# A four-layer graph network on one core: layer 0 loads x transposed and takes its means off there

## The chip, the core and the metric

One core of one Trainium2 chip runs the whole program. The metric is the device time of one execution in microseconds (us); lower is better. The kernel before has a median of 1261.44 us in three runs (1258.7 to 1262.8).

## What is computed

x holds 128 graphs of 128 nodes with 256 features in fp32, and adj one 128x128 adjacency matrix with ones on its diagonal. Four layers follow one another, each of them x = x + layer(relu(layernorm(x))):

```python
# layer 0                                   a = adj as float, deg = a.sum(axis=1)
out = deg * (h @ Wi.T + b) + a @ (h @ Wj.T)
# layer 1                                   Wh = h @ W
logits = leaky_relu(Wh @ a_src + (Wh @ a_dst).T); out = softmax(masked logits) @ Wh
# layer 2                                   the same with 128 columns, and h itself beside it
# layer 3                                   8 heads of 32: softmax(masked q @ k.T / sqrt(32)) @ v, then @ Wo.T + bo
```

Layernorm has no weights: (x - mean) / sqrt(var + 1e-5) over the 256 features. Adjacency is the same for all graphs.

## The kernel before

The graphs are worked on in 64 pairs (G = 2); p is the number of a pair. A pair passes through some 120 operations on five engines. Each engine runs `step(t)` for t from -31 on, and in it a fixed list of operations, each on pair t - LAG[operation]. An operation waits by semaphores for what it reads, for the readers of the buffer it overwrites (`read_before`), and on TensorE for the earlier readers of its PSUM bank (`bank_free`, from the table BANKS). Nothing else orders the engines: each takes its list strictly in order, so one that waits holds up all that stands behind it in its list. LAG counts list rounds of an engine by itself, not time.

Layer 0 of a pair, in order: SyncE loads x (`load`). VectorE takes statistics (`stats0`, L486, and `mv0`, L495). GpSimd makes var + eps, its power -0.5 and the negative mean (`veps0` L311, `rstd0` L327, `nm0` L317), and the normalised rows `y0` (L335, two instructions). TensorE transposes them in four pieces of 128x128 (`h0t`, L911) into one bank. ScalarE applies relu and rounds to fp32r (`h0t_hi`, L726), and VectorE keeps what the rounding left (`h0t_lo`, L524). TensorE multiplies by both weights with three products each (`m0`, `m1`, L901 to L903). ScalarE and VectorE split the neighbours' half the same way (`mj_hi` L732, `mj_lo` L502), VectorE adds deg times the own half to x + deg * b (`t0_0`, `t0_1`, L509; GpSimd's `r0`, L343), and TensorE multiplies by the adjacency (`s0`, L930), after which VectorE sums (`x1`).

Layer 1 needs the products with a_dst along a row. GpSimd gathers the column (`dst1`, L358) once ScalarE has copied the projections (`wh0`, `wh1`, L738). SyncE writes it to DRAM (`row_out1`, L251: rows<-dst) and, when that has landed, reads it back spread over all partitions (`row_in1`, L257: db<-rows). ScalarE then forms the logits (`z1`, L764), VectorE masks them (`nmax1`, L534), ScalarE takes the exponentials (`exp1`, L773), TensorE transposes them (`e1t`, L966), ScalarE copies (`at1`, L781), and TensorE attends (`x2_mm`, L974). Layer 2 has the same round through DRAM (`dst2`, `row_out2`, `row_in2`, `z2`). The first four and last five pairs go without DRAM: TensorE spreads the column by two transposes of a broadcast column (`d1`, `d2`, L958).

ScalarE's list before, from `z1` on: z1, ht2, p3t_0, p3t_2, p3t_3, exp1, hh, h1t_hi, exp3_3, at1, ot_hi, h0t_hi, exp3_1, wh0, wh1, p3t_1, h3t_hi, v, z2, mj_hi1, exp3_2, exp2, mj_hi0, exp3_0, at2, and z1 of the next pair. `exp3_*` are four exponentials each (L795), `p3t_*` copies of 128x512 (L803), `ot_hi` one of 128x512 (L809).

SyncE's list before: row_in1, row_out2, row_in2, load (L239), row_out1, store (L244). All of its DMAs are on one queue.

Of the kernel before, what the change touches and what calls it, by code (L numbers as in the profile page):

```python
# [29 lines left out]
       "row_in1": 1, "row_out2": 2, "row_in2": 2, "load": -4, "row_out1": 0, "store": 7, "x4_mm": 7, "products": 0, "m1": -1, "qt_mm": 4, "m0": -1,  # L30
       "kt_mm": 4, "e2t": 3, "d1": 1, "pt0": 6, "h2t": 2, "pt2": 6, "x3_mm": 3, "pt3": 6, "hh_mm": 2, "h1t": 0, "scores": 4, "adj_spread": -31,
       "ot_mm": 6, "e1t": 1, "pt1": 5, "h0t": -2, "x2_mm": 1, "wh0_mm": 0, "wh1_mm": 0, "v_mm": 4, "h3t": 3, "d2": 2, "s0": -1, "exp3_1": 5, "wh0": 1,
       "wh1": 1, "p3t_1": 6, "h3t_hi": 4, "v": 5, "w3_high": 0, "z2": 3, "w0_high": -9, "mj_hi1": -1, "exp3_2": 5, "exp2": 3, "mj_hi0": -1,
       "exp3_0": 5, "at2": 3, "z1": 1, "ht2": 2, "p3t_0": 6, "p3t_2": 6, "p3t_3": 6, "exp1": 1, "hh": 2, "h1t_hi": 0, "exp3_3": 5, "at1": 1,
       "ot_hi": 6, "h0t_hi": -2, "qt": 5, "t0_1": 0, "rsum2": 4, "stats0": -2, "mj_lo0": 0, "rsum3_1": 6, "rsum3_2": 6, "kt": 5, "rsum3_0": 6,
       "nmax1": 2, "x3": 4, "t0_0": 0, "stats3": 4, "mv3": 4, "w0_low": -1, "rsum1_any": 2, "h1t_lo": 1, "nmax3_1": 5, "adj_rows": -29, "nmax3_2": 5,
       "mv0": -2, "nmax3_0": 5, "rsum3_3": 6, "h0t_lo": -1, "ot_lo": 7, "x2": 2, "nmax3_3": 5, "stats2": 2, "h3t_lo": 4, "mv2": 2, "x1": 0,
       "nmax2": 3, "x4": 7, "stats1": 0, "mv1": 0, "w1_split": 0, "mj_lo1": -1, "y3": 4, "r0": -2, "dst1": 1, "w3_low1": 1, "w3_low3": 2, "veps0": -2,
       "nm0": -2, "p3_0": 6, "rstd0": -2, "p3_3": 6, "veps2": 2, "nm2": 2, "deg_b_made": -23, "rstd2": 2, "y2": 2, "w3_low2": 1, "veps1": 0, "r3": 5,
       "nm1": 0, "rstd1": 0, "y1": 0, "x3_tail": 3, "p3_2": 5, "p3_1": 5, "y0": -2, "dst2": 2, "veps3": 3, "nm3": 3, "w3_low0": 2, "rstd3": 3,  # L40
       "rsum1": 1,
# [4 lines left out]
    "x4b": (6, "x4_mm", ('x4',)),  # L46
    "prep": (4, "products", ('w1_split',)),
    "m1": (0, "m1", ('mj_lo1', 't0_1')),
    "qt": (1, "qt_mm", ('qt',)),
    "m0": (5, "m0", ('mj_lo0', 't0_0')),  # L50
    "kt": (6, "kt_mm", ('kt',)),
    "at2": (2, "e2t", ('at2',)),
    "d1": (4, "d1", ('z1',)),
    "pt0": (0, "pt0", ('p3t_0',)),
    "h2t": (1, "h2t", ('ht2',)),
    "pt2": (3, "pt2", ('p3t_2',)),
    "x3b": (2, "x3_mm", ('x3',)),
    "pt3": (4, "pt3", ('p3t_3',)),
    "hh": (6, "hh_mm", ('hh',)),
    "h1t": (3, "h1t", ('h1t_lo',)),  # L60
    "sc0": (1, "scores", ('nmax3_0',)),
    "sc1": (2, "scores", ('nmax3_1',)),
    "sc2": (5, "scores", ('nmax3_2',)),
    "sc3": (0, "scores", ('nmax3_3',)),
    "prepa": (0, "adj_spread", ('adj_rows',)),
    "ot": (4, "ot_mm", ('ot_lo',)),
    "at1": (6, "e1t", ('at1',)),
    "pt1": (3, "pt1", ('p3t_1',)),
    "h0t": (2, "h0t", ('h0t_lo',)),
    "x2b": (6, "x2_mm", ('x2',)),  # L70
    "wh0": (5, "wh0_mm", ('wh0',)),
    "wh1": (1, "wh1_mm", ('wh1',)),
    "v": (2, "v_mm", ('v',)),
    "h3t": (5, "h3t", ('h3t_lo',)),
    "d2": (4, "d2", ('z2',)),
    "x1b": (3, "s0", ('x1',)),
# [6 lines left out]
BUFFERS = {"x0": 2, "y0": 2, "ht0": 2, "mj": 2, "t0": 2, "r0": 2, "x1": 2, "y1": 2, "ht1": 2, "wh": 2, "z1": 2, "e1": 2, "at1": 2, "x2": 2, "y2": 2, "ht2": 2, "hh": 2, "z2": 2, "e2": 2, "at2": 2, "x3": 2, "y3": 2, "ht3": 2, "kt": 2, "qt": 2, "v": 2, "r3": 2, "exps3": 1, "probs3": 1, "probs3t": 1, "ot": 2, "x4": 2, "masked3": 1}  # L83


def gnn_kernel(nc, x, adj, w0t, bias0, w1, w1t, a1, w2, w2t, a2, wqt, bq, wkt, bk, wvt, bv, wot, bo, out):
# [7 lines left out]
    with ExitStack() as ctx:  # L94
# [44 lines left out]
        y = [sb("y0", [P, BUFFERS["y0"], G, D]), sb("y1", [P, BUFFERS["y1"], G, D]), sb("y2", [P, BUFFERS["y2"], G, D]), sb("y3", [P, BUFFERS["y3"], G, D])]  # L139
# [25 lines left out]
        nm = [sb(f"nm{i}", [P, SMALL, G]) for i in range(4)]  # L165
# [20 lines left out]
        x_in = [sem(f"x_in{i}") for i in range(BUFFERS["x0"])]  # L186
        x_out = [sem(f"x_out{i}") for i in range(BUFFERS["x4"])]


        S = {name: sem(name) for name in LAG if name not in ("row_in1", "row_out2", "row_in2", "load", "row_out1", "store")}  # L190
# [44 lines left out]
        def _(sp):  # L235
            def load(p):
                b = p % BUFFERS["x0"]
                read_before(sp, "x0", p, "y0", "r0")
                sp.dma_start(x0[:, b], x_pairs[bass.ds(p, 1)].rearrange("o n g d -> (o n) g d")).then_inc(x_in[b], 16)  # L239

            def store(p):
                b = p % BUFFERS["x4"]
                passed(sp, "x4", p)
# [15 lines left out]
            def step(t):  # L259
# [6 lines left out]
                if due(t, "load") and t - LAG["load"] >= 2:  # L266
                    load(t - LAG["load"])
# [870 lines left out]
```

## Time and profile before

| | us |
|---|---|
| median of three runs (1258.7 to 1262.8) | 1261.44 |
| span of the profiled execution | 1270.7 |
| TensorE matmuls busy | 1244.1 (98%) |
| VectorE busy | 1073.1 (84%) |
| GpSimd busy | 1066.2 (84%) |
| ScalarE busy | 1042.1 (82%) |

The profiled execution's own time is its span; no time around it is recorded. It is 9.3 us, or 0.7%, above the median of the runs that were not profiled. TensorE's rows give for each matmul the time from its start to a modelled end; matmuls overlap, so the time that one costs is read from one start to the next, not from its duration. In the timeline and in the table of lines, "idle before" is what the engine waited directly before that instruction, and the name behind the arrow is what ended it.

### The profile page before, as it was taken

What the parts mean: (1) busy time and instruction counts of PE and PEld (TensorE: products, weight loads), DVE (VectorE), ACT (ScalarE), POOL (GpSimd) and SP (SyncE); (2) the same over time, 40 slices, a digit from 0 to 9 for tenths busy, and PEclk for the clock granted to TensorE, in tenths of its full rate; (3) what the DMA queues carried; (4) which work ended last, traced back from release to release, by engine and by line L of the source; (5) the groups of instructions that cost most, each with busy time, mean ns of one, the idle gap of its engine ahead of it and who ended that gap; (6) DMA issues with size and microseconds to landing.
All of it is one profiled execution on the core that took longest, in us unless ns stands there. A gap on an engine that the chain in (4) does not pass through costs nothing. (4 is left out here: it accounts for less than half of the span.)

```text
span 1270.7 us, 43666 instructions
## 1 busy us (share of the span) xinstructions
PE 1244.1 (98%) x12253; PEld 1143.5 (90%) x12253; DVE 1073.1 (84%) x5137; ACT 1042.1 (82%) x3911; POOL 1066.2 (84%) x1914
## 2 busy tenths in 40 slices
PE   8899999999999999999999999999999999999997
PEld 6789999999999999999899999899999989999986
DVE  5788888888988888888888888888988888888883
ACT  3578888888888888888788888788888888898996
POOL 6879888888888888888788888889888888887773
PEclk8999999999999999999999999999999999999998
DMA  4011221222222321221211222322222312211000
GB/s 127 26 23 22 52 43 36 52 36 43 52 39 40 52 45 35 51 47 32 52 32 47 48 35 48 48 34 50 48 36 47 48 31 52 48 27 31 19 19 34
DMA packets 70604, 53.59 MB, mean 42 GB/s; under 512 B 20704, under 2 KB 70368, under 8 KB 70368
## 3 DMA queue, kind: packets, MB, share of 16 engines
q1 hardware_dynamic: 67888, 49.09, 20.0%
q8 instruction: 104, 1.70, 0.7%
q14 instruction: 132, 1.08, 0.6%
q10 hardware_dynamic: 2480, 1.71, 0.5%
HBM read 33.89 MB, written 16.89 MB: 40 GB/s over the span
## 5 line engine op out<-in xcount | busy, mean ns | idle before, releaser
L795 ACT ACTIVATE exps<-masked,nmax 128x128 f32<-128x128 f32 x1024 | 397.5, 398 | 0.0
L335 POOL TENSOR_SCALAR y<-x,nm,rstd 128x256 f32<-128x256 f32 x512 | 281.0, 557 | 23.4 <-issue 21.8
L364 POOL TENSOR_TENSOR probs<-exps,rsum 128x512 f32<-128x512 f32 x256 | 263.5, 1041 | 10.4 <-PE bank L1019 5.6
L577 DVE CUSTOM_DVE_ANT_0 masked<-bank,mask 128x128 f32<-128x128 f32 x1024 | 227.8, 284 | 2.9 <-PE bank L1011 2.8
L795 ACT ACTIVATION_READ_ACCUMULATOR exps<-masked,nmax 128x1 f32 x1024 | 202.3, 198 | 0.0
L486 DVE BATCH_NORM_STATS2 stats<-x 128x6 f32<-128x256 f32 x512 | 190.8, 414 | 8.7 <-DMA x<-in_x 7.2
L901 PE MATMUL bank<-w_hi,ht_hi 128*128 128x512 f32 (+1 forms) x512 | 187.7, 367 | 2.1 <-DVE ht_lo L524 2.1
L327 POOL TENSOR_TENSOR rstd<-veps,power 128x2 f32<-128x2 f32 x256 | 182.8, 714 | 0.1
L524 DVE SCALAR_TENSOR_TENSOR ht_lo<-bank,ht_hi 128x512 fp32r<-128x512 f32 x192 | 131.0, 682 | 57.1 <-ACT ht_hi L726 56.8
L903 PE MATMUL bank<-w_hi,ht_lo 128*128 128x512 f32 (+1 forms) x512 | 175.6, 343 | 0.0
L902 PE MATMUL bank<-w_lo,ht_hi 128*128 128x512 f32 (+1 forms) x512 | 175.3, 342 | 0.0
L726 ACT ACTIVATE ht_hi<-bank 128x512 fp32r<-128x512 f32 x192 | 115.8, 603 | 71.3 <-PE bank L911 66.0
L911 PE MATMUL bank<-ident,y 128*128 128x128 f32 x1024 | 156.3, 275 | 5.0 <-POOL y L335 3.2
L1019 PE MATMUL bank<-ident,probs 128*128 128x128 f32 x1024 | 153.2, 273 | 0.6 <-DVE t L509 0.6
L803 ACT ACTIVATE probs3t<-bank 128x512 f32<-128x512 f32 x256 | 137.9, 595 | 3.4 <-PE bank L1019 3.4
L732 ACT ACTIVATE mj_hi<-bank 128x256 fp32r<-128x256 f32 x128 | 49.2, 384 | 103.0 <-PE bank L903 95.7
L911 PEld LDWEIGHTS bank<-ident,y 128*128 128x128 f32 x1024 | 116.2, 141 | 16.4 <-issue 6.4
L1019 PEld LDWEIGHTS bank<-ident,probs 128*128 128x128 f32 x1024 | 119.9, 141 | 2.0 <-issue 2.0
L903 PEld LDWEIGHTS bank<-w_hi,ht_lo 128*128 128x128 f32 x512 | 97.7, 191 | 12.1
L901 PEld LDWEIGHTS bank<-w_hi,ht_hi 128*128 128x128 f32 x512 | 97.8, 191 | 10.7 <-DVE ht_lo L524 2.6
L902 PEld LDWEIGHTS bank<-w_lo,ht_hi 128*128 128x128 f32 x512 | 97.5, 190 | 8.6
L311 POOL TENSOR_SCALAR veps<-mv 128x2 f32<-128x2 f32 x256 | 59.2, 231 | 52.2 <-DVE mv L495 31.5
(122 smaller groups left out, 3737.5 us busy)
## 6 DMA issues: line engine op xcount, KB each, us to landing
x<-in_x SPq DMA_DIRECT2D x64, 256.0 KB, 5.0
out<-x SPq DMA_DIRECT2D x64, 256.0 KB, 6.2
db<-rows SPq DMA_DIRECT2D x110, 128.0 KB, 4.1
rows<-dst SPq DMA_DIRECT2D x110, 1.0 KB, 4.1
probs<-in_w0t ACTq DMA_DIRECT2D x1, 256.0 KB, 5.6
probs<-in_w0t SPq DMA_DIRECT2D x1, 256.0 KB, 6.7
probs<-in_w1t ACTq DMA_DIRECT2D x1, 256.0 KB, 6.7
exps<-in_wot SPq DMA_DIRECT2D x1, 256.0 KB, 7.4
```

Of the source, the lines that this page charges most:

```text
L327: pool.tensor_tensor(rstd[i][:, b], veps[i][:, b], power[:], ALU.pow).then_inc(S[f"rstd{i}"], 1)
L335: last = pool.tensor_scalar(y[i][:, b, g], src[:, bx, g], nm[i][:, s, g:g + 1], rstd[i][:, s, g:g + 1], ALU.add, ALU.mult)
L364: pool.tensor_tensor(probs3[:, p % BUFFERS["probs3"], j], exps3[:, p % BUFFERS["exps3"], j], rsum3[:, s, j].unsqueeze(2).to_broadcast([P, ...
L486: last = dve.bn_stats(stats[i][:, b, g], src[:, bx, g])
L577: last = dve.tensor_tensor_reduce(masked3[:, b, j, i], bank_of(f"sc{j}")[:, i * P:(i + 1) * P], mask[:], scale=-1.0, scalar=-MASKED, op0=A ...
L795: last = act.activation(exps3[:, b, j, i], masked3[:, p % BUFFERS["masked3"], j, i], ACT.Exp, bias=nmax3[:, s, j, i:i + 1], scale=-1.0, ac ...
L803: act.activation(probs3t[:, b, j].rearrange("p b n -> p (b n)"), bank_of(f"pt{j}")[:], ACT.Copy).then_inc(S[f"p3t_{j}"], 1)
L901: pe.matmul(out_ap, lhs[0], rhs[0], start=start, stop=False)
L902: pe.matmul(out_ap, lhs[0], rhs[1], start=False, stop=False)
L903: return pe.matmul(out_ap, lhs[1], rhs[0], start=False, stop=stop)
L911: last = pe.transpose(bank_of(f"h{i}t")[:, (c * G + g) * P:(c * G + g + 1) * P], y[i][:, b, g, c * P:(c + 1) * P], ident[:])
L1019: last = pe.transpose(bank_of(f"pt{j}")[:, i * P:(i + 1) * P], probs3[:, p % BUFFERS["probs3"], j, i], ident[:])
```

## The change

The host passes x a second time, transposed (`xt`: for each pair 128 partitions of features, 2 x 2 x 128 values). SyncE loads it for each pair (`loadt`, 256 KB). TensorE no longer transposes `y0`; its `h0t` is now two transposes of a broadcast column of means, which puts the mean of node n in column n of every partition. VectorE subtracts them from the transposed x (`d0s`, two instructions of 128x256). `h0t_hi` and `h0t_lo` read the difference in SBUF instead of PSUM. The factor rstd, which is positive and belongs to a node, is taken out of the relu: it comes in as a scale per partition in `mj_hi`, as a factor in `mj_lo` (a scalar_tensor_tensor in place of a tensor_tensor), and as deg * rstd in `t0_*` (a new small GpSimd operation, `degr`). `nm0` and `y0` are gone. The buffer y0 goes, xt gets two buffers, x0 a third.

```diff
-"x0": 2, "y0": 2,
+"x0": 3, "xt": 2,
+            def load_transposed(p):
+                b = p % BUFFERS["xt"]
+                read_before(sp, "xt", p, "h0t_hi", "h0t_lo")
+                sp.dma_start(xt_sb[:, b], xt[bass.ds(p, 1)].rearrange("o p c g n -> (o p) c g n")).then_inc(xt_in[b], 16)
...
+            def spread_means(p):
+                passed(pe, "mv0", p)
+                bank_free(pe, "h0t", p)
+                for g in range(G):
+                    last = pe.transpose(bank_of("h0t")[:, g * P:(g + 1) * P], mv[0][:, p % SMALL, g, 0:1].to_broadcast([P, P]), ident[:])
+                last.then_inc(S["h0t"], 1)
...
+            def subtract_means(p):
...
+                for c in range(DC):
+                    last = dve.tensor_tensor(xt_sb[:, b, c], xt_sb[:, b, c], means, ALU.subtract)
+                last.then_inc(S["d0s"], 1)
...
+            def relu_difference_high(p):
...
+                act.activation(ht0_r[0][:, b].rearrange("p c g n -> p (c g n)"), xt_sb[:, bx].rearrange("p c g n -> p (c g n)"), ACT.Relu).then_inc(S["h0t_hi"], 1)
...
-                act.activation(mj_r[0][:, b, g], bank_of(f"m{g}")[:, D:2 * D], ACT.Copy).then_inc(S[f"mj_hi{g}"], 1)
+                act.activation(mj_r[0][:, b, g], bank_of(f"m{g}")[:, D:2 * D], ACT.Copy, scale=rstd[0][:, p % SMALL, g:g + 1]).then_inc(S[f"mj_hi{g}"], 1)
...
-                dve.scalar_tensor_tensor(t0[:, b, g], bank_of(f"m{g}")[:, 0:D], deg[:], r0[:, p % BUFFERS["r0"], g],
+                dve.scalar_tensor_tensor(t0[:, b, g], bank_of(f"m{g}")[:, 0:D], degr[:, p % SMALL, g:g + 1], r0[:, p % BUFFERS["r0"], g],
```

All five lists, LAG and BANKS are drawn anew. The lists after, where the prediction speaks of them:

- TensorE: x2_mm, wh0_mm, pt1, wh1_mm, v_mm, h3t, s0, h0t, x4_mm, m1, qt_mm, kt_mm, m0, e2t, h2t, pt2, pt0, x3_mm, hh_mm, h1t, pt3, e1t, scores, ot_mm. Before, h0t stood between pt1 and x2_mm.
- ScalarE from z1 on: z1, at2, ht2, p3t_2, p3t_0, mj_hi0, exp1, hh, h1t_hi, p3t_3, at1, exp3_3, ot_hi, h0t_hi, exp3_1, wh0, wh1, p3t_1, v, h3t_hi, z2, exp3_2, exp2, exp3_0, mj_hi1.
- SyncE: row_in1, row_out2, row_in2, loadt, row_out1, store, load.
- GpSimd has veps3 and nm3 ahead of dst2 (before: behind it); VectorE has nmax1 as the last of its list, and low_w0 two rounds ahead of the first d0s. The bank of wh1 is the one that ot had before it.

## Rows read from the trace of the kernel before

**Rows 1.** The page, busy time (share of the span) and instructions by engine

```profile
PE 1244.1 (98%) x12253; PEld 1143.5 (90%) x12253; DVE 1073.1 (84%) x5137; ACT 1042.1 (82%) x3911; POOL 1066.2 (84%) x1914
```

**Rows 2.** Timeline, TensorE, `s0`: start us, us, engine line operation

```profile
150.82 0.48 PE L930 MATMUL bank<-mj_hi,aggr_r 128*128 128x512 f32 x1
...
1144.62 0.48 PE L930 MATMUL bank<-mj_hi,aggr_r 128*128 128x512 f32 x1
```

**Rows 3.** Groups of lines, TensorE, 150 to 1144 us: xcount | busy, mean ns

```profile
L930 PE MATMUL bank<-mj_hi,aggr_r 128*128 128x512 f32 x52 | 24.9, 478 | 0.0
```

**Rows 4.** Timeline, TensorE: pt1, h0t, x2_mm; later h2t and pt2

```profile
602.51 0.60 PE L1019 MATMUL bank<-ident,probs 128*128 128x128 f32 x4
603.03 0.63 PE L911 MATMUL bank<-ident,y 128*128 128x128 f32 x4
603.50 1.03 PE L974 MATMUL bank<-wh,at 128*128 128x256 f32 x4
...
615.89 0.60 PE L911 MATMUL bank<-ident,y 128*128 128x128 f32 x4
616.33 0.60 PE L1019 MATMUL bank<-ident,probs 128*128 128x128 f32 x4
```

**Rows 5.** Timeline, ScalarE, one pair's z1 to the next pair's

```profile
885.30 0.68 ACT L764 ACTIVATE bank<-db,wh 128x128 f32<-128x128 f32 x2
...
890.87 0.39 ACT L781 ACTIVATE at<-bank 128x256 f32<-128x256 f32 x1
...
891.14 0.61 ACT L809 ACTIVATE ot_hi<-bank 128x512 fp32r<-128x512 f32 x1
...
891.84 0.60 ACT L726 ACTIVATE ht_hi<-bank 128x512 fp32r<-128x512 f32 x1
...
892.33 0.39 ACT L795 ACTIVATE exps<-masked,nmax 128x128 f32<-128x128 f32 x1
...
893.88 0.65 ACT L738 ACTIVATE wh<-bank 128x258 f32<-128x258 f32 x2
...
904.19 0.68 ACT L764 ACTIVATE bank<-db,wh 128x128 f32<-128x128 f32 x2
```

**Rows 6.** Timeline, SyncE's queue, the DMA issues beside rows 5

```profile
889.55 0.32 SPq L251 DMA_DIRECT2D rows<-dst  x1
892.55 0.32 SPq L257 DMA_DIRECT2D db<-rows  x1
892.97 0.39 SPq L239 DMA_DIRECT2D x<-in_x  x1
894.80 0.32 SPq L251 DMA_DIRECT2D rows<-dst  x1
...
900.18 0.32 SPq L257 DMA_DIRECT2D db<-rows  x1
```

**Rows 7.** Lines L251 (rows<-dst), then L257 (db<-rows): issue to landing, both layers

```profile
DMA to landing us min/median/max: 2.6/4.1/8.1
...
DMA to landing us min/median/max: 2.8/4.1/7.7
```

**Rows 8.** Groups of lines: xcount | busy, mean ns | idle before, releaser

```profile
L764 ACT ACTIVATE bank<-db,wh 128x128 f32<-128x128 f32 x110 | 37.3, 371 | 7.1 <-DMA db<-rows 6.9
...
L795 ACT ACTIVATE exps<-masked,nmax 128x128 f32<-128x128 f32 x1024 | 397.5, 398 | 0.0
...
L732 ACT ACTIVATE mj_hi<-bank 128x256 fp32r<-128x256 f32 x128 | 49.2, 384 | 103.0 <-PE bank L903 95.7
...
L509 DVE SCALAR_TENSOR_TENSOR t<-bank,deg,r 128x256 f32<-128x256 f32 x128 | 60.7, 474 | 0.0
...
L502 DVE TENSOR_TENSOR mj_lo<-bank,mj_hi 128x256 fp32r<-128x256 f32 x128 | 51.4, 401 | 5.5 <-ACT mj_hi L732 5.2 <-issue 0.2
```

**Rows 9.** Timeline of the start: VectorE's low part of w0, TensorE's first layer-0 product

```profile
10.46 1.35 DVE L460 TENSOR_TENSOR w_lo<-probs,w_hi 128x1024 fp32r<-128x1024 f32 x1
...
12.60 0.79 PE L901 MATMUL bank<-w_hi,ht_hi 128*128 128x512 f32 x1 [1.73 <-DVE ht_lo L524]
```

## What the change does to the time: the prediction

> **What bounds the kernel now.** I read the busy table first. TensorE is busy for 98% of the span [rows 1], so the first question is whether each pair costs its matmuls alone. The start of `s0` gives the period: 52 of them lie between 150.82 and 1144.62 us [rows 2, 3], so a pair takes 993.8 / 52 = 19.11 us on average. The second view is a step without a disturbance: `z1` starts at 885.30 and again at 904.19 [rows 5], 18.89 us later. So TensorE's work sets about 18.9, and 0.2 us per pair comes from elsewhere. The table of lines says where a part of it is: before `z1` ScalarE waits 6.9 us for db<-rows [rows 8], over 55 pairs that go through DRAM 0.13 each. The third view is that round itself. ScalarE takes 893.88 - 885.30 = 8.58 us from `z1` to the next pair's `wh` copies, and then 904.19 - 893.88 = 10.31 to the next `z1` [rows 5]. In those 10.31 us the column goes out and back: issue of rows<-dst 0.92 after `wh`, db<-rows issued 5.38 later [rows 5, 6], and its landing. ScalarE has other work for 10.31 us, so the round is hidden as long as it is shorter. It is a loop: `z1` of a pair, then `wh` of the next, then its round, then its `z1`; nothing in an in-order list lets a later pair pass. Its length is only just under TensorE's.
>
> **The change part by part.**
>
> *TensorE.* The old `h0t` and `pt1` ahead of it took 603.50 - 602.51 = 0.99 us, where four transposes without a wait take 0.44 (615.89 to 616.33) [rows 4]. So old `h0t` costs 0.99 - 0.44 = 0.55, of which 0.11 is a wait. The new one has half as many, 0.22, and stands between `s0` and `x4_mm`. Saved: 0.33 us per pair; TensorE's period becomes 18.89 - 0.33 = 18.56. A bound on the other side: if the wait turns up at the new place, 0.22 are saved.
>
> *ScalarE, from `z1` to `wh`.* Counted along both lists, the new stretch has one `at` copy and one `mj_hi` more, and nothing less. An `at` copy takes 0.27 (890.87 to 891.14) [rows 5]; I take the same for `mj_hi`, which has the same size. `ot_hi` took 0.70 to the next instruction, where the same size takes 0.49 (891.84 to 892.33) [rows 5]; the 0.21 was a wait for the transposes of `h0t`, which `h0t_hi` no longer depends on there. So 8.58 + 0.27 + 0.27 - 0.21 = 8.91; if the wait stays, 9.12. `mj_hi` now takes its scale from a column. No row has that, but the exponentials, which take a column as bias, last 398 ns for 128 elements, while `mj_hi` without one lasts 384 for 256 [rows 8]; a column thus costs something between 0 and 0.15 us. I take 0.1 and get 9.0. Above that, `wh1_mm` now waits for the bank that VectorE's `ot_lo` empties, which can add 0 to 0.3; I leave it in the range.
>
> The Trainium skill ("ScalarE: Activation LUTs", section "What ACT_TABLE_LOAD costs") says that each [128,1] pointer operand adds about 93 ns to an activation, which speaks against this change. By it the stretch is an estimated 9.0 too; with no such price it would be 8.9.
>
> *The round through DRAM.* Its order on SyncE's queue stays: the column of layer 2 out and in, a load of 256 KB, the column of layer 1 out. What was `load` there is now `loadt`, and the new `load` comes behind `store`, between rows<-dst and db<-rows. Rows<-dst without a load ahead landed in 3.0 (889.55 to 892.55), the one 1.8 us behind the load in 5.38 [rows 6]; that stays, as the size of the load does. For db<-rows I take 3.5, between the shortest and the median [rows 7]. The round from `wh` to `z1` is then 0.92 + 5.38 + 3.5 = 9.8. The waits in rows 8 show that in a part of the steps it passes 10.31, so the mean is a little above: 10.0, with 9.6 and 10.6 as bounds (landings go from 2.6 to 8.1 [rows 7]). GpSimd now has `veps3` and `nm3` ahead of `dst2`, which holds layer 2's column and what SyncE has queued behind it (`loadt`, then layer 1's rows<-dst) until `mv3` is done; I leave 0 to 0.3 for it.
>
> *The sum of the loop.* 9.0 + 10.0 = 19.0 us. That is above TensorE's new 18.56 and close to the old mean of 19.11. Before, ScalarE's work covered 10.31 us of the round; now, were TensorE to run at 18.56, it would cover 18.56 - 9.0 = 9.56, less than the round. So most of what TensorE saves turns into a wait of ScalarE at `z1`, and of TensorE at `e1t` behind it.
>
> *VectorE.* Busy 1073.1 us [rows 1], 16.8 per pair. `d0s` adds two operations of 128x256 from PSUM and SBUF, like `mj_lo` at 401 ns: 0.80. `mj_lo` becomes the form of `t0` at 474 [rows 8]: twice 0.07. `h0t_lo` reads SBUF instead of PSUM; taken at nothing, within 0.1 either way. Together 17.7 per pair, which a period of 18.56 still holds.
>
> *GpSimd* loses the two `y0` and `nm0` and gains the small `degr`. It is off the loop but for `dst1`, which waits for ScalarE, so I count nothing. *SyncE* issues one DMA more per pair, behind whose wait for `h0t_lo` of two pairs earlier stands rows<-dst; that reader runs a round earlier, so no cost. *Loads*: `d0s` needs xt some 7 us after its issue by the lists; if it is late, VectorE's whole list waits.
>
> *Start and end.* At the start the first `d0s` stands behind `low_w0` on VectorE, which runs from 10.46 for 1.35 [rows 9]. Where `h0t_lo` followed, `d0s` (0.8) and `h0t_hi` (0.6) now come first, so the first product moves from 12.60 [rows 9] by about 1.4; between -1 and 3, as the means need no GpSimd. The nine pairs at the two ends have no round and save TensorE's 0.33 each: 3.0.
>
> *The sum.* Against the profiled execution: 55 x (19.0 - 19.11) = -6, ends -3, start +1.4, together -8, so 1263 of its 1270.7. The median lies 9.3 lower than that execution. If unprofiled runs have the same landings, the median becomes 1261.4 - 8 = 1254. If their landings are shorter, the old kernel had few waits left (19.11 - 9.3 / 55 = 18.94), and the new one gains from each tenth: with a round of 9.7 it has 18.7, so 55 x -0.24 - 2 = -15 and 1246. With 10.0 and an old period of 18.94 it is +3 - 2, so 1263. I forecast **1254 us**, with 1246 to 1264 as this case's own range.
>
> **Rivals.**
>
> *TensorE's floor is reached.* If the round is at most 9.5 us (xt comes in longer runs per partition than x), the loop is hidden and a pair takes 18.56. Against the unprofiled 18.94 that is 55 x -0.38 = -21, with ends and start -23: 1238. For it speaks that rows<-dst alone needs only 3.0 [rows 6]; against it, that the load ahead of it stays.
>
> *The round gets longer, and the kernel slower.* The new `load` is issued between rows<-dst and db<-rows. Both layers' landings spread from 2.6 to 8.1 us [rows 7], and in rows 6 the longer one is that with a load ahead. If it adds 0.5 to the mean, the loop is 9.0 + 10.5 = 19.5, or 55 x 0.3 to 0.5 = +17 to +28: about 1282. It decides from a round of 9.95 on, where loop and unprofiled old period are equal (9.0 + 9.95 = 18.95). The Trainium skill ("DMA: Bandwidth & Descriptors", section "Queues, rings and completion order") states that a completion's semaphore write lands only after every earlier write of that DMA engine; by this rule db<-rows would wait for the new load's data as well. Rows 6 agree for the load ahead of rows<-dst (5.38 against 3.0).
>
> *VectorE becomes the bound.* It had 19.11 - 16.8 = 2.3 us of idle time per pair. At 17.7 of work, 0.9 are left at 18.56. If its list needs 1.6 of waiting, a pair takes 19.3: 55 x 0.2 against the profile, about 1270. For it speaks that `nmax1`, its last entry, waits for `z1`; against it, that it keeps 1.3 at 19.0.
>
> *The change does less than it says* on TensorE: if the wait of 0.11 moves along, the floor is 18.67. That shifts the first rival by 6 us and not the loop.
>
> **How the numbers follow.** The loop as worked out: 0.45 (1246 to 1264). TensorE's floor: 0.20 (1236 to 1246). The longer round: 0.22 (1264 to 1290). VectorE: 0.13 (1260 to 1280). A measurement of this kernel can tell about 0.3%, 3.8 us, from no change. Faster than 1257.7: 0.20 of the floor and 0.30 of the loop, 0.50. Within 1257.7 to 1265.2: 0.13 of the loop, 0.03 and 0.03 of the last two, 0.19. Slower: 0.31. For 8 in 10 I leave out a tenth at either side: 1238 to 1282.
>
> **What would show it.** Right, if in the profile after, `z1` starts directly after its db<-rows in nearly every step, ScalarE's idle time before L764 (db,wh) is 0.5 us or more per pair instead of 0.13, `z1` to `wh` takes 9.0, `e1t` becomes TensorE's main wait, and the period is 19.0. Wrong towards faster, if that wait is small and the period is 18.6. Wrong towards slower, if rows<-dst or db<-rows of layer 1 lands clearly later than 5.4 and 3.5, or if VectorE is without idle time or waits for xt at `d0s`.

## The result and the profile after

| | median us | range of runs | ratio to before, 95% interval |
|---|---|---|---|
| before | 1262.1 | 1258.7 to 1263.1 | |
| after | 1381.3 | 1380.4 to 1382.9 | 1.095 [1.093, 1.097] |

The change makes the kernel 9.5% slower. The forecast was 1254 us with a range up to 1282, so the direction was wrong and the time lies 99 us outside the range. The profiled execution of after has a span of 1379.6 us.

The busy table of after, in the columns of [rows 1], shows TensorE at 91% of the span where it was at 98%. It has 128 matmuls fewer to do than before; what is new is that it waits.

```profile
PE 1256.4 (91%) x12125; PEld 1132.7 (82%) x12125; DVE 1128.0 (82%) x5265; ACT 1071.8 (78%) x3911; POOL 991.6 (72%) x1786
```

The start of `s0` gives the pair again, beside [rows 2]: 46 pairs lie between these two rows, so a pair takes 976.3 / 46 = 21.22 us, where it was 19.11.

```profile
153.06 0.48 PE L988 MATMUL bank<-mj_hi,aggr_r 128*128 128x512 f32 x1
...
1129.40 0.48 PE L988 MATMUL bank<-mj_hi,aggr_r 128*128 128x512 f32 x1
```

The view of waits of the kernel after names what is late (engine, line, what it waited for: us in total, times, longest). The lines are VectorE's, ScalarE's, TensorE's and GpSimd's largest:

```profile
DVE x L642 <- DMA out<-x: 172.6, 53, 5.2
...
ACT bank L815 <- DMA db<-rows: 177.2, 109, 3.7
...
PE bank L952 <- DVE x L642: 61.4, 50, 2.6
...
POOL r L375 <- DVE x L642: 135.4, 53, 4.0
```

The first line is new. L642 is `x4`, the last sum of a pair. It writes one of two buffers, and what that buffer held, the output of two pairs earlier, must have been stored. In the kernel before nothing waited for a store; here `x4` does so in 53 pairs, for 3.3 us each. The third and fourth line are its echo: TensorE's products wait for the bank that `x4` empties, and GpSimd for its sum. The second line is the wait that the prediction looked for, ScalarE at `z1` and `z2`.

The groups of lines of after (count | busy us, mean ns | idle before, and its releaser) answer to [rows 8] and give the new operations' own durations:

```profile
L815 ACT ACTIVATE bank<-db,wh 128x128 f32<-128x128 f32 x110 | 37.6, 374 | 102.4 <-DMA db<-rows 102.4
...
L783 ACT ACTIVATE mj_hi<-bank,rstd 128x256 fp32r<-128x256 f32 x128 | 59.8, 467 | 15.9 <-PE bank L954 15.9
...
L551 DVE TENSOR_TENSOR xt_sb<-xt_sb,bank 128x256 f32<-128x256 f32 x128 | 46.2, 403 | 0.3 <-PE bank L969 0.3
...
L525 DVE SCALAR_TENSOR_TENSOR mj_lo<-bank,rstd,mj_hi 128x256 fp32r<-128x256 f32 x128 | 60.8, 475 | 3.4 <-ACT mj_hi L783 3.1
...
L558 DVE SCALAR_TENSOR_TENSOR ht_lo<-xt_sb,ht_hi 128x512 fp32r<-128x512 f32 x64 | 83.8, 1309 | 0.0
```

Before `z1` ScalarE now waits 102.4 us where it was 6.9. The subtraction (403 ns) and `mj_lo` (475 ns) cost what was forecast. The low part of `h0`, L558, takes 1309 ns; the same work took 682 ns in the kernel before, where one operand came from PSUM.

One stretch of the timeline of after shows the first wait from inside (start us, us, engine line operation; SyncE's issues, then VectorE, then ScalarE):

```profile
702.90 2.01 SPq L248 DMA_DIRECT2D xt_sb<-in_xt  x1
705.00 0.38 SPq L260 DMA_DIRECT2D rows<-dst  x1
705.44 0.42 SPq L253 DMA_DIRECT2D out<-x  x1
705.95 0.42 SPq L243 DMA_DIRECT2D x<-in_x  x1
710.68 0.33 SPq L266 DMA_DIRECT2D db<-rows  x1
...
725.59 0.63 SPq L260 DMA_DIRECT2D rows<-dst  x1
726.27 0.42 SPq L253 DMA_DIRECT2D out<-x  x1
...
712.17 0.69 DVE L642 TENSOR_TENSOR x<-bank,r 128x512 f32<-128x512 f32 x1 [4.03 <-DMA out<-x]
...
724.46 0.74 ACT L789 ACTIVATE wh<-bank 128x258 f32<-128x258 f32 x2
```

The store goes out at 705.44, directly behind layer 1's rows<-dst. `x4` starts at 712.17, 6.7 us later, after 4.03 us without work. Everything behind `x4` on VectorE is late with it, and so is what needs that: the `wh` copy of the next round (724.46), its rows<-dst (725.59), and the store that stands behind it (726.27). That closes a loop. Its four parts, as means of 42 pairs in the trace: store to `x4` 7.28, `x4` to `wh` 12.35, `wh` to rows<-dst 1.19, rows<-dst to store 0.46; the sum is 21.28 us. Such a sum is the pair in any kernel, since each part starts where the last one ends. That the store holds the pair here is seen at `x4`: in 52 of the 53 pairs that wait it starts 0.12 us after the landing of the store that it waits for (0.49 in the other).

The other loop, the prediction's, in the same way. The table has means of 42 pairs in the middle of each trace, in us; the kernels under after are the experiments below. "db issue" is the issue of layer 1's db<-rows. Here too the sum is the pair whatever holds it. The round through DRAM can hold the pair only where `z1` has to wait for its db: `z1` starts within 0.3 us of that landing in 42 of 43 pairs in after and in all 43 in a1_store12, but in 23 of 43 in before.

| kernel | z1 to wh | wh to rows<-dst | rows<-dst to db issue | db issue to z1 | sum |
|---|---|---|---|---|---|
| before | 8.58 | 1.01 | 5.75 | 3.79 | 19.12 |
| after | 10.16 | 1.17 | 6.36 | 3.56 | 21.25 |
| a1_store12 | 9.01 | 1.11 | 6.10 | 3.48 | 19.69 |
| a2_row_first | 9.03 | 0.97 | 5.14 | 4.57 | 19.70 |
| c1_loadt | 9.05 | 0.97 | 5.62 | 3.71 | 19.35 |
| a4_transfers | 9.29 | 0.98 | 3.96 | 4.57 | 18.80 |
| a5_low_later | 9.33 | 0.96 | 3.92 | 4.53 | 18.75 |
| a9_after_z1 | 9.63 | 0.96 | 4.00 | 4.18 | 18.76 |
| b3_store (before's operations) | 8.57 | 0.97 | 4.14 | 5.24 | 18.93 |

### The profile page after: what moved, and what is told of

It is laid out like the page before. It is cut to its first block and busy times, and to the rows that moved or that the text cites. A ratio compares the mean times of both kernels' runs of the same rounds, so it can differ in the third digit from the quotient of the medians.

```text
span 1379.6 us, 43844 instructions
## 1 busy us (share of the span) xinstructions
PE 1256.4 (91%) x12125; PEld 1132.7 (82%) x12125; DVE 1128.0 (82%) x5265; ACT 1071.8 (78%) x3911; POOL 991.6 (72%) x1786
## 3 DMA queue, kind: packets, MB, share of 16 engines
q14 instruction: 135, 1.11, 0.5%
## 5 line engine op out<-in xcount | busy, mean ns | idle before, releaser
L952 PE MATMUL bank<-w_hi,ht_hi 128*128 128x512 f32 (+1 forms) x512 | 198.4, 388 | 63.1 <-DVE x L642 61.4
L619 DVE CUSTOM_DVE_ANT_0 masked<-bank,mask 128x128 f32<-128x128 f32 x1024 | 232.5, 283 | 5.8 <-PE bank L1069 4.7
L359 POOL TENSOR_SCALAR y<-x,nm,rstd 128x256 f32<-128x256 f32 x384 | 210.1, 554 | 22.9 <-issue 21.5
L642 DVE TENSOR_TENSOR x<-bank,r 128x512 f32<-128x512 f32 x64 | 44.2, 691 | 178.1 <-DMA out<-x 172.6
L375 POOL TENSOR_TENSOR r<-x,c 128x512 f32<-128x512 f32 x64 | 82.8, 1294 | 135.5 <-DVE x L642 135.4
L854 ACT ACTIVATE probs3t<-bank 128x512 f32<-128x512 f32 x256 | 145.6, 596 | 10.6 <-PE bank L1077 8.6
L1077 PE MATMUL bank<-ident,probs 128*128 128x128 f32 x1024 | 145.8, 276 | 6.1
L962 PE MATMUL bank<-ident,y 128*128 128x128 f32 x768 | 116.8, 275 | 1.7 <-POOL y L359 1.7
L815 ACT ACTIVATE bank<-db,wh 128x128 f32<-128x128 f32 x110 | 37.6, 374 | 102.4 <-DMA db<-rows 102.4
L824 ACT ACTIVATE ez<-z,nmax 128x128 f32<-128x128 f32 x256 | 100.2, 395 | 3.8 <-DVE nmax L576 2.6
```

What stands on the lines that cost most here:

```text
L359: last = pool.tensor_scalar(y[i][:, b, g], src[:, bx, g], nm[i][:, s, g:g + 1], rstd[i][:, s, g:g + 1], ALU.add, ALU.mult)
L619: last = dve.tensor_tensor_reduce(masked3[:, b, j, i], bank_of(f"sc{j}")[:, i * P:(i + 1) * P], mask[:], scale=-1.0, scalar=-MASKED, op0=A ...
L854: act.activation(probs3t[:, b, j].rearrange("p b n -> p (b n)"), bank_of(f"pt{j}")[:], ACT.Copy).then_inc(S[f"p3t_{j}"], 1)
L952: pe.matmul(out_ap, lhs[0], rhs[0], start=start, stop=False)
L962: last = pe.transpose(bank_of(f"h{i}t")[:, (c * G + g) * P:(c * G + g + 1) * P], y[i][:, b, g, c * P:(c + 1) * P], ident[:])
L1077: last = pe.transpose(bank_of(f"pt{j}")[:, i * P:(i + 1) * P], probs3[:, p % BUFFERS["probs3"], j, i], ident[:])
```

## The experiments

Three theories stood at the start. The first: the new SyncE list issues the store one pair later against rows<-dst, and `x4` pays for it. The second: the DRAM round of layer 1 became too long by itself. The third: VectorE, with the longer low part, is the bound.

**a1_store12: the store one round earlier.**

```diff
-"row_out1": 5, "store": 13, "load": -1,
+"row_out1": 5, "store": 12, "load": -1,
```

> The changed kernel with one number altered: in SyncE's list the store of a pair is issued one round earlier (lag 12 in place of 13), so that it no longer stands behind the layer-1 row write of the pair six later. Theory 1 (the store's place): VectorE's sum x4 waits 172.6 us for stores in the profile of after, 53 times, 3.3 us a pair; with the store a round earlier the wait is gone, the pair falls from 21.2 us to 19.0 to 19.5 us, and the time to 1255 to 1290 us. Theory 2 (the DRAM round of layer 1 is too long by itself: 10.2 us from z1 to wh, 11.1 us from wh back to z1): the store's place is a symptom, the pair stays at 21 us or above and the time at 1365 us or above. Theory 3 (VectorE at 17.6 us of work a pair, grown by the low part of h0 at 1.35 us): the wait only moves to another instruction, the pair stays near 20.5 us, 1330 to 1350 us.

1302.9 us, ratio to before 1.034 [1.033, 1.036]. The wait for the store is gone; VectorE's and ScalarE's largest waits are now:

```profile
DVE z L576 <- ACT bank L815: 48.1, 60, 1.9
...
ACT bank L815 <- DMA db<-rows: 160.3, 110, 3.2
```

So the store's place cost 78 us: the largest part, as the first theory has it, but not all. What is left is 44 us above before, a little more than that theory's 1255 to 1290. ScalarE still waits 160 us for db, 101 of them before `z1` (group of lines):

```profile
L815 ACT ACTIVATE bank<-db,wh 128x128 f32<-128x128 f32 x110 | 37.6, 374 | 101.0 <-DMA db<-rows 101.0
```

From `z1` to `wh` it has no idle stretch of over 0.05 us in the middle pairs. So the pair of 19.69 us waits for the round through DRAM, and for the rest the second theory holds, though its own numbers (21 us a pair, 1365 us or above) missed.

**a6_three_x4: the same wait taken away by a buffer, with no order changed.**

```diff
-"ot": 2, "x4": 2, "masked3": 1
+"ot": 2, "x4": 3, "masked3": 1
```

> The changed kernel with a third buffer for x4 and nothing else altered: the store keeps its late place in SyncE's list, but x4 overwrites what was stored three pairs earlier, not two. Theory (x4 waits because the store of two pairs earlier is issued only some 4 us before): the wait of x4 for stores (172.6 us in after) is gone without any change of order, and the time is that of a1_store12, 1295 to 1315 us. If the late store itself slows the pair (its bytes beside the row writes), the time stays above 1340 us with the wait gone.

1299.5 us, 1.031 [1.028, 1.034], and the first of VectorE's waits is the same as in a1_store12:

```profile
DVE z L576 <- ACT bank L815: 43.8, 58, 2.2
```

Two different edits that have only the wait in common give the same time. It was the reuse of the buffer that cost 78 to 82 us, and not the bytes of the store at that place.

**a2_row_first: a1, and rows<-dst of layer 1 ahead of the transposed load.**

```diff
-                if due(t, "loadt") and t - LAG["loadt"] >= 2:
-                    load_transposed(t - LAG["loadt"])
                 if due(t, "row_out1") and not at_an_end(t - LAG["row_out1"]):
                     write_row(1, t - LAG["row_out1"])
+                if due(t, "loadt") and t - LAG["loadt"] >= 2:
+                    load_transposed(t - LAG["loadt"])
```

> As a1_store12, and in SyncE's list the layer-1 row write is issued ahead of the transposed load, whose issue takes 1.3 to 2.0 us of the queue in the profile of after. If with the store out of the way the DRAM round of layer 1 sets the pair, this shortens it by 1 to 1.5 us: the wait of z1 for db falls below 0.5 us a pair (102.4 us over 55 pairs in after) and the time is 15 to 50 us below a1_store12. If something else sets the pair there (TensorE's own 18.6 us, or VectorE), both are within 5 us of one another.

1300.1 us, 1.033 [1.032, 1.035]: nearly a1's time. That looks like the expectation's second case, but the table says otherwise. The part from rows<-dst to the db issue fell by 0.96 us, as wanted, and the part from there to `z1` rose by 1.09. Three transfers of 256 KB stood between row write and row read, and what the write no longer waited for, the read met.

**c1_loadt and a4_transfers: the large transfers out of the round.** In c1_loadt (from a1) the transposed load alone goes right behind the db read of layer 1; in a4_transfers (from after, the store's lag back at 13, the lag of load at 0 in place of -1) all three go there. The cut shows a4_transfers without its lags and without the lines at the old places.

```diff
                 if due(t, "row_in1") and not at_an_end(t - LAG["row_in1"]):
                     spread_row(1, t - LAG["row_in1"])
+                if due(t, "store"):
+                    store(t - LAG["store"])
+                if due(t, "loadt") and t - LAG["loadt"] >= 2:
+                    load_transposed(t - LAG["loadt"])
+                if due(t, "load") and t - LAG["load"] >= 2:
+                    load(t - LAG["load"])
                 if due(t, "row_out2") and not at_an_end(t - LAG["row_out2"]):
```

> As a1_store12, with the transposed load alone moved behind the layer-1 db read; store and load of x stay between rows<-dst and db<-rows. If the new load is what lengthened the layer-1 DRAM round (6.1 us from rows<-dst to the issue of db in a1_store12, 5.7 us in before, 4.0 us in a4_transfers with all three moved): this falls to 5.2 to 5.7 us, the pair from 19.7 to 19.0 to 19.3 us, and the time to 1265 to 1280 us. If store and load of x do the harm, it stays at 6.0 us and 1295 to 1303 us.

> The changed kernel with its three 256 KB transfers a pair (store, transposed load, load of x) issued together right after the layer-1 db read in SyncE's list, where the profile of a2_row_first leaves the queue empty for some 9.5 us, and no longer between rows<-dst and db<-rows of layer 1. Theory (what is left after a1 and a2, 41 to 44 us over before, is the DRAM round of layer 1 with the large transfers inside it): from rows<-dst to the issue of db falls from 5.1 to about 4.5 us, from there to z1 from 4.6 to about 3.6 us; with 9.0 us from z1 to wh and 1.0 us to rows<-dst the loop is 18.1 us, under TensorE's floor of 18.6 us (the shortest pairs of a2_row_first are 18.61 to 18.67 us), so 18.6 to 18.9 us a pair and 1235 to 1255 us. Rival (VectorE with the doubled low part of h0, 17.8 us of work a pair, or the order of the lists): the pair stays at 19.3 us or above, 1280 to 1300 us, even without a wait for db.

c1_loadt: 1281.6 us, 1.018 [1.015, 1.021], just past the end of its range. a4_transfers: 1257.2 us, 0.998 [0.996, 0.999]. From a1_store12 the transposed load takes back 21 us by leaving the round, and store and load of x together another 24. In the table rows<-dst to db falls from 6.10 to 5.62 and to 3.96, while the part from there to `z1`, expected at 3.6, rises to 4.57. ScalarE's idle time ahead of `z1` in a4_transfers, to set beside the 102.4 us of after:

```profile
L815 ACT ACTIVATE bank<-db,wh 128x128 f32<-128x128 f32 x110 | 37.7, 374 | 49.5 <-DMA db<-rows 49.5
```

The time is 2 us above what the theory expected, as some pairs still take over 19 us; the rival that VectorE or the lists hold the pair above 19.3 us falls: the mean is 18.80.

**a5_low_later: a4, and the low part of h0 behind its neighbour on VectorE.**

```diff
-                if due(t, "h0t_lo"):
-                    relu_difference_low(t - LAG["h0t_lo"])
...
                 if due(t, "x2"):
                     sum_x2(t - LAG["x2"])
+                if due(t, "h0t_lo"):
+                    relu_difference_low(t - LAG["h0t_lo"])
```

> As a4_transfers, with two neighbours on VectorE swapped: the low part of h0, read from SBUF, comes after the sum x2 in place of before it, so that it starts about 0.8 us later, when GpSimd's probabilities (1.04 us, from 716.88 in the stretch of a2_row_first where the low part runs from 717.10) are nearly over. Theory (the low part is held up while GpSimd runs its two-operand product): its mean falls from 1.35 us towards 0.68 us, to 0.7 to 1.0 us. Rival (reading from SBUF is slow by itself): it stays at 1.35 us. On the time: if VectorE is not the bound, within 5 us of a4_transfers; if it is, up to 30 us below.

1254.1 us, 0.995 [0.994, 0.997], 3 us below a4_transfers, whose interval it overlaps. The line L558, first in after and then in a5_low_later (count: duration ns min/median/max, first and last start us):

```profile
L558 DVE SCALAR_TENSOR_TENSOR ht_lo<-xt_sb,ht_hi x64: 657/1370/1800, 13.7 to 1270.8; 128x512 fp32r<-128x512 f32 x64
```

```profile
L558 DVE SCALAR_TENSOR_TENSOR ht_lo<-xt_sb,ht_hi x64: 657/682/1825, 13.7 to 1142.1; 128x512 fp32r<-128x512 f32 x64
```

Its median is 682 ns again, with both operands still in SBUF. What changed is GpSimd's neighbour. In the timeline of after the low part starts 0.22 us behind the product for the probabilities; in that of a5_low_later it starts when that product (711.27 + 1.04) is over:

```profile
723.31 1.37 DVE L558 SCALAR_TENSOR_TENSOR ht_lo<-xt_sb,ht_hi 128x512 fp32r<-128x512 f32 x1
...
723.09 1.04 POOL L388 TENSOR_TENSOR probs<-exps,rsum 128x512 f32<-128x512 f32 x1
```

```profile
712.29 0.68 DVE L558 SCALAR_TENSOR_TENSOR ht_lo<-xt_sb,ht_hi 128x512 fp32r<-128x512 f32 x1
...
711.27 1.04 POOL L388 TENSOR_TENSOR probs<-exps,rsum 128x512 f32<-128x512 f32 x1
```

So the low part stands still while GpSimd runs that product. The third theory's operation is real and its price is real (0.63 us a pair), but VectorE was not the bound, and the time hardly moves.

Two `s0` rows of a5_low_later, one pair apart, show an undisturbed pair: 431.48 - 412.88 = 18.60 us. The line below them is the view of windows for just that pair (its length; then busy us and instructions of TensorE, its weight loads, VectorE, ScalarE and GpSimd; granted clock; DMA). TensorE is busy all the time and VectorE for 17.00 us of it, so TensorE's own work sets it.

```profile
412.88 0.48 PE L988 MATMUL bank<-mj_hi,aggr_r 128*128 128x512 f32 x1
...
431.48 0.48 PE L988 MATMUL bank<-mj_hi,aggr_r 128*128 128x512 f32 x1
...
412.88:431.48 18.60, 18.60 (x191) 17.30 (x190) 17.00 (x83) 16.36 (x62) 15.32 (x29) 1.00 0.22 59
```

**a3_no_dram: a1 without any round through DRAM.**

```diff
-BY_TRANSPOSE = (4, 5)
+BY_TRANSPOSE = (64, 0)
```

> As a1_store12, but no pair sends its dst row through DRAM: all 64 use the transposes on TensorE that the first 4 and the last 5 use in after. That adds four transposes of 128 columns a pair, about 0.75 to 1.1 us of TensorE (273 ns each in the profile, overlapping), and takes away both DRAM rounds with their DMAs and waits. If only the DRAM rounds and the store held the pair, it falls to TensorE's floor, 18.6 + 0.8 = 19.4 us, 1270 to 1290 us. If VectorE or the order of the lists holds it too, it stays above 20 us, over 1310 us.

1273.3 us, 1.011 [1.009, 1.013]; nearly every pair takes 19.06 to 19.26 us, a little less than the 19.4 that was expected and 0.6 us less than in a1_store12, though TensorE has four transposes more a pair. So neither VectorE nor the new lists hold the pair above that.

**b2_transfers and b3_store: the kernel before with the same medicine.** In b2_transfers store and load go right behind the db read, in b3_store the store alone; the cut shows b3_store without the lines at the old place.

```diff
                     spread_row(1, t - LAG["row_in1"])
+                if due(t, "store"):
+                    store(t - LAG["store"])
```

> Control: the kernel before with its store and its load moved in the same way, right behind the layer-1 db read. The loop of before has 5.7 us from rows<-dst to the issue of db, with the store right behind the row write; without it some 4.5 us, so the loop falls below the 18.9 us of TensorE's own work. If that holds, the pairs of 19.2 to 20.5 us that stand among those of 18.9 us go, and the time is 5 to 15 us below before (1245 to 1255 us); if the store does not touch the round, it is within 3 us of before.

> Control: the kernel before with its store alone moved right behind the layer-1 db read (in b2_transfers the load went with it and SyncE sat behind it, 470 us waiting for GpSimd's y to free the buffer of x). If the store lengthens the layer-1 round of before: from rows<-dst to the issue of db falls from 5.7 to 4.0 to 4.8 us, the pairs of 19.2 to 20.5 us go, all stand at 18.9 us, TensorE's floor there, and the time is 1245 to 1255 us. If not, it is within 3 us of before. Either way it tells what the changed operations are worth beside a5_low_later when both have their transfers out of the round: TensorE's 0.3 us a pair over 55 pairs is 16 us.

b2_transfers: 1275.8 us, 1.013 [1.010, 1.015], slower, where 5 to 15 us of gain were expected. SyncE's own waits say why: `load` needs the buffer that GpSimd's `y0` reads, and at the new place SyncE sits there, with layer 2's row write behind it.

```profile
SPq L239 <- POOL y L335: 470.0, 61, 10.3
```

So b2_transfers is no clean control. b3_store is: 1259.6 us, 1.000 [0.999, 1.001]. The expected gain of 5 to 15 us did not come either, but the round did what was expected: rows<-dst to db fell from 5.75 to 4.14 us. The load still stands ahead of the row write, and is still under way when that is issued, in all 42 pairs; only the store behind it is gone. One round in SyncE's timeline, to set beside [rows 6]:

```profile
920.60 0.39 SPq L239 DMA_DIRECT2D x<-in_x  x1
922.65 0.32 SPq L251 DMA_DIRECT2D rows<-dst  x1
926.81 0.32 SPq L257 DMA_DIRECT2D db<-rows  x1
```

Its idle time before `z1` has vanished (group of lines), and all but one of its middle pairs take 18.89 to 18.94 us (two `s0` rows of the timeline):

```profile
L764 ACT ACTIVATE bank<-db,wh 128x128 f32<-128x128 f32 x110 | 37.0, 368 | 0.1
```

```profile
374.74 0.48 PE L930 MATMUL bank<-mj_hi,aggr_r 128*128 128x512 f32 x1
...
393.67 0.48 PE L930 MATMUL bank<-mj_hi,aggr_r 128*128 128x512 f32 x1
```

That the time is unchanged suggests that the kernel before runs at TensorE's floor already when it isn't profiled, and that the longer pairs of its profiled execution (span 1270.7) are hardly there in its other runs (median 1259.8 on this chip); no pair of those runs is on record. Set beside a5_low_later, the changed operations with their transfers out of the round gain 18.92 - 18.60 = 0.3 us in a steady pair, and 5.5 us over the whole run.

**h2_old_lists and h3_sub_later: the changed operations in the lists of before.** h3_sub_later differs from h2_old_lists only in the place of the subtraction:

```diff
-                if due(t, "d0s"):
-                    subtract_means(t - LAG["d0s"])
                 if due(t, "nmax3_0"):
                     mask_scores(0, t - LAG["nmax3_0"])
+                if due(t, "d0s"):
+                    subtract_means(t - LAG["d0s"])
```

> The change's operations without its new lists: the lists, lags and banks of the kernel before, with the transposed load after the store on SyncE, the scaled degree after rstd0 on GpSimd, the subtraction right after the layer-0 mean on VectorE, the high part of h0 on ScalarE after wh1 instead of ahead of it, and the low part on VectorE after the last masked scores. If the loss is in the new lists (theory 1): no x4 wait, TensorE saves its 0.33 us a pair and ScalarE's stretch from z1 to wh loses the 0.6 us of the high part, so 18.6 to 19.0 us a pair and 1235 to 1260 us. If the new operations themselves cost it (the subtraction's 0.80 us and 0.67 us more for the low part on VectorE, the transposed load on SyncE's queue), it stays above 20 us a pair, 1320 us or more.

> As h2_old_lists, with VectorE's subtraction behind the masked scores that stand after it there. Reading of h2_old_lists: its pairs are all 19.5 us, with no wait for db; its chain goes ScalarE's high part, VectorE's masked scores, the subtraction (0.8 us), the last masked scores, which free the bank of TensorE's second wh product, so the subtraction sits on the loop. If so, the pair falls by 0.5 to 0.8 us, to 18.7 to 19.0 us, 1260 to 1275 us. If VectorE's work as such (18.0 us a pair) is the bound, the pair stays at 19.4 to 19.6 us, about 1306 us.

h2_old_lists: 1306.7 us, 1.038 [1.036, 1.040]; the expectation of 1235 to 1260 missed, and so did the other case's 1320 or more. Its middle pairs are all 19.5 us, and ScalarE has no wait for db, so no transfer holds them. In its timeline the subtraction stands ahead of the last masked scores, and TensorE waits for these to empty a bank (the matmul at 706.63 starts when the scores' maximum at 706.40 is read):

```profile
704.92 0.72 DVE L550 TENSOR_TENSOR xt_sb<-xt_sb,bank 128x256 f32<-128x256 f32 x2
705.55 0.29 DVE L618 CUSTOM_DVE_ANT_0 masked<-bank,mask 128x128 f32<-128x128 f32 x1
...
706.40 0.09 DVE L618 DVE_READ_ACCUMULATOR2_ANT nmax<- 128x1 f32 x1
...
706.63 0.36 PE L951 MATMUL bank<-w_hi,ht_hi 128*128 128x258 f32 x1 [0.43 <-DVE nmax L618]
```

h3_sub_later: 1269.5 us, 1.008 [1.006, 1.010]; the pair falls to 18.86 us, inside what was expected. The move also shortened the low part, from a mean of 1349 to 801 ns, as it now meets GpSimd's product for a shorter time; which of the two gave the 0.65 us isn't told apart. That its total stays above a5_low_later's comes from the mean pair, 18.90 against 18.75, and from the first eight pairs, which end 6.7 us later (`s0` of the ninth pair at 138.8 against 132.0).

**a9_after_z1: a5, and the transfers wait until z1 has used db.**

```diff
                     spread_row(1, t - LAG["row_in1"])
+                    passed(sp, "z1", t - LAG["row_in1"])
```

> As a5_low_later, but SyncE issues its three large transfers only when z1 has used the layer-1 db, not right behind the read of db. In a5_low_later the steady pairs are 18.60 to 18.64 us, TensorE's floor, and the mean is 18.75; z1 and z2 still wait 92.5 us for db. If the transfers beside the db read cause that: from the issue of db to z1 falls from 4.5 to about 3.5 us, nearly all pairs stand at 18.6 us, and the time is 3 to 8 us below a5_low_later, 1246 to 1251 us. Rival: the transfers now run beside the layer-2 round instead (its row write comes some 5.5 us after z1), z2 waits in place of z1, and the time is 1253 to 1260 us.

1250.5 us, 0.992 [0.991, 0.994], the lowest ratio of all. From the issue of db to `z1` it is 4.18 in place of 4.53 us, a smaller fall than expected. ScalarE's idle time before `z1` falls from 45.9 to 27.1 us, and before `z2` it rises from 46.7 to 49.7. Of 48 pairs in the middle 33 are below 18.7 us, where a5_low_later has 29, but the mean is the same (18.74 against 18.75). The medians differ by 3.6 us, the spans of the two profiled executions by 1.2; in these two the ninth `s0` comes 3.6 us earlier here (128.5 against 132.0), and the stretch behind the last `s0` is 2.7 us longer. That it is faster than before is measured, and the time lies where the theory put it; that it is so for the reason given isn't shown, as the mean pair did not move.

## Why the prediction was wrong, step by step

**The step that failed** is the one on SyncE: "*SyncE* issues one DMA more per pair [...] so no cost". It followed what the new load holds up, and put the store at nothing without a word, though the new lists moved that too: from lag 7 beside a `row_out1` of lag 0 to lag 13 beside lag 5, one pair later. Two rows more would have priced it. In the trace of before a store is issued 22.4 us before the `x4` that reuses its buffer (mean of 42; one case in the timeline below, and the stores' time to landing), and lands in 6.2 (median), so it has 16.2 us to spare.

```profile
646.50 0.43 SPq L244 DMA_DIRECT2D out<-x  x1
...
669.08 0.69 DVE L600 TENSOR_TENSOR x<-bank,r 128x512 f32<-128x512 f32 x1
...
DMA to landing us min/median/max: 2.1/6.2/8.2
```

One pair later takes 19.1 of that: the buffer comes 2.9 us late, and the profile of after has 3.3. What the runs show in place of no cost is 172.6 us of waiting at `x4`, and 78 to 82 us of time that come back when it goes (a1_store12, a6_three_x4). How 2.9 us of lateness turn into that price can't be worked out from before; the pairs measured with and without the wait, 21.28 and 19.69 us, differ by 1.6, which over 53 pairs is 84 us.

**The DRAM round** was the right second bound, and its size was off. ScalarE's stretch from `z1` to `wh` was forecast at 9.0 and is 9.01 in a1_store12. The round was forecast as 0.92 + 5.38 + 3.5, taken at 10.0, and is 1.11 + 6.10 + 3.48 = 10.7. The term that was too small is rows<-dst's landing, "that stays, as the size of the load does". Of its 0.72 us, about half was there before the change: 5.38 is one step of [rows 6], where the mean of before is 5.75. The other 0.35 came with the change, which puts the load of x behind the row write, beside the store. The prediction also put the length down to the wrong neighbour. It read 5.38 against 3.0 as the price of the load ahead; b3_store, with the load still ahead and the store gone from behind, has 4.14. In the changed kernel the transfer ahead costs 0.48 (6.10 to 5.62 in c1_loadt), and the two behind it 1.66 more (to 3.96 in a4_transfers). That was the rival of the longer round, at 1282. Its mechanism, the new load behind rows<-dst, is a part of what a1_store12, c1_loadt and a4_transfers show. Its loop of 19.5 was 0.2 short, its own figures give +21 to +31 us (19.5 less 19.11 or 18.94, over 55 pairs) where it has +17 to +28, and with the store's wait gone the kernel stands at 1303.

The Trainium skill ("DMA: Bandwidth & Descriptors", section "Queues, rings and completion order") says that a semaphore write waits for every earlier write of its DMA engine. The order of landings agrees: in before, after, a1_store12 and b3_store the row lands after the large transfer issued ahead of it in all 42 pairs, by 0.16 us at least. The rule alone does not give the lengths, for what is issued behind the row write counts too: 3.96 us without large transfers close to it, 4.14 with one ahead, 5.14 with three behind, 5.62 with two behind, 6.10 with one ahead and two behind. By what means those behind slow it, no run shows.

**VectorE.** The subtraction (forecast 401 ns each, measured 403), `mj_lo` (474, 475) and the scale from a column (0.1 us for `mj_hi`, measured 467 - 384 = 83 ns) were right. "`h0t_lo` reads SBUF instead of PSUM; taken at nothing, within 0.1 either way" was wrong by 0.63 us. The Trainium skill has the rule that the step should have used ("SBUF — State Buffer", section "SBUF: two separate sides"): a VectorE operation with two SBUF inputs and a GpSimd operation that reads SBUF exclude one another. The runs agree with it in the direction and nearly in the size (below). It changed little: in a4_transfers VectorE still has 1.19 us of idle time in a mean pair, and only the 3 us of a5_low_later came back, within the noise.

**TensorE and the kernel before.** The forecast of TensorE's floor, 18.56 us, is borne out: a5_low_later's undisturbed pairs are 18.60 to 18.64. That the median of before hides a pair of 18.94 fits b3_store (18.92, with the median of before). The first rival, the floor reached at 1238, needs the transfers out of the round; with a4_transfers, a5_low_later and a9_after_z1 it comes to 1250 to 1257. In a5_low_later the mean pair is still 0.15 us above the floor, 8 us over 55 pairs. Its cause stays open: in a9_after_z1 ScalarE waits 19 us less before `z1`, and the mean pair is the same. The first product starts at 14.44 us, 1.8 later than in [rows 9] where 1.4 was forecast.

## What to carry to other kernels

When the lists of a pipelined kernel are drawn anew, go through every transfer that moved, old ones first: take from the trace the time from its issue to the next writer of its buffer, subtract its landing and the shift, and see whether anything is left. A small transfer on which a loop depends is worth a stretch of the queue without large ones, and a queue's idle stretch is easily found in its timeline. When the parts of a loop are added up, look for a wait at each link: the sum alone is the period of any kernel. A fix for one kernel (the load behind the db read) can be a loss in another with one buffer less and a later reader, so the wait of the moved transfer has to be looked up there too.

## What the hardware showed unasked

VectorE's operation with both inputs in SBUF stands still while GpSimd multiplies two SBUF operands. In h2_old_lists 56 of 64 low parts overlap such a product, and duration less overlap is 547.6 ns with a spread of 1.0; the shortest, without overlap, takes 691. So all but some 0.14 us of it is shut out. The exclusion works the other way too. In the same trace GpSimd's power function, which takes 0.71 us elsewhere, takes 1.17 where it starts in the second half of a low part:

```profile
708.68 1.44 DVE L557 SCALAR_TENSOR_TENSOR ht_lo<-xt_sb,ht_hi 128x512 fp32r<-128x512 f32 x1
...
708.53 1.04 POOL L387 TENSOR_TENSOR probs<-exps,rsum 128x512 f32<-128x512 f32 x1
709.53 1.17 POOL L342 TENSOR_TENSOR rstd<-veps,power 128x2 f32<-128x2 f32 x1
```

An issue on SyncE isn't always short. The 256 KB transfer that is issued directly behind a db read takes over 1 us to issue in 12 of 56 cases in after (2.01 us at 702.90 above), whichever transfer it is: in before it is the load of x, over 1 us in 13 of 55, and in a5_low_later the store, in 22 of 54. At their places in after, store and load of x take 0.38 to 0.43 us in the middle pairs. In a9_after_z1 the store has the same neighbour in the list but is issued only when `z1` has used what that read brought, and 0 of 54 take over 0.43 us. So the long issues go with a db read that is still under way; what the queue waits for then, no run here shows.
